# The z projection of a gated linear attention, from one pass over float32 operands to three over their float32r halves

## The chip, the cores and the metric

One core of one Trainium2 chip runs the whole program. The time is device microseconds of one execution; the kernel before has a median of 1250.59 us over 3 runs (1248.19 to 1251.07).

## What is computed

Two transformer layers over x of 4 x 256 tokens (T = 1024) and 256 channels. The change lies in the attention of the first layer, which has 16 heads of 128:

```python
q = _silu(x @ Wq); k = _silu(x @ Wk); v = _silu(x @ Wv)
z = x @ Wz                       # the change is here
q, k, v = (_causal_dwconv(u, w) for ...)     # 4 taps
# rotary, norms of q and k, 4 lags of q.k_s * sigmoid(a_s * b) * v_s
out = out * rms * norm_w * _silu(z)
return out @ Wout
```

Behind it come a feed-forward layer with weights from a table of 16 values, a second attention (softmax, 4-bit codes with scales) and a mixture of 32 experts.

## The kernel before

The program is written by hand, one instruction stream for each engine, with semaphores between them. Nothing plans the order: each stream runs as it stands in the code.

**Heads and turns.** The first attention goes head by head. `turns0` (line 350) calls `turn` on every engine; a turn of head h does part 1 (projections and convolutions of head h), part 2 (the scores and the sum over lags of head h-1) and part 3 (gate and store of head h-2). Two turns stand ahead of a hardware loop of 7 x 2, two or three behind it. The weights of one head are one tile `wh[par]` of 128 x 1024: four blocks q, k, v, z of KC x 128 = 256 columns.

**Two kinds of product.** TensorE multiplies a stationary tile (loaded first, the PEld rows of the profile) with moving columns. q, k and v are made channel by channel: stationary is a 128x128 block of weights, moving are 512 tokens. They go by halves: ScalarE writes the upper half of a tile as float32r (`upper0`, line 908: `w_hi`), VectorE subtracts it from the tile and so gets the lower half (`lower0`, line 1160: `w_lo`, in place over `wh`), the input has its two halves `hh_h` and `hh_l` once for all heads, and `by_halves` (lines 519 to 523) issues three products for one: low x high, high x low, high x high. These are lines 521, 522, 523 in the profile, whoever calls them.

z is made token by token: stationary is a 128x128 block of the input `h_t`, moving are the 128 columns of the z weights, for 8 blocks of tokens and KC = 2 halves of the channels, 16 float32 products for a head (line 609). The profile shows two records (a load and a multiplication each) for each float32 product, and one for each float32r product. z's columns of `wh` are no part of the halves: `w_hi` and `w_lo` hold QKV = 768 of the 1024 columns.

**TensorE's order in a turn**, with what it waits for: squared sums of k of head h-1 (line 576), k (waits for silu of z of the head before), the gate's transposes (595), v, a transpose of sums (604), z (609; waits for `a0_silu_k`), the transposes of v of head h-1 (616), its scores (624), squared sums of q (576), then `project_q` of head h+1, which waits for `a0_w_lo`, `a0_silu_v` and `a0_v_tok` (ScalarE has copied slot 0 of PSUM out, line 967), and last the products with the band (640, 644).

**ScalarE's order in a turn**: store of head h-2 (932, 938), silu and first tap of k (914, 924), 944, silu and tap of v, `upper0` of head h+1 (908), squares of q and k (955; wait for their convolutions), silu of z (959; waits for `a0_z`), `v_tok` of head h-1 (967; waits for the transposes of v and `a0_rqk`), silu and tap of q of head h+1.

**VectorE's order in a turn**: gate (1188), 1193, convolution of q (1171, three times), 1200 (waits for the transpose of line 604), convolution of k, `lower0` of head h+1 (1160), convolution of v, the band (1213, 1216), four rotary products (1177, 1183).

SyncE reloads `wh[par]` for head h+2 after `a0_z` of head h, and loads the table's indices after the last `a0_z`; they lie over `hh_h` and `hh_l`.

Of the kernel before, what the change touches and what calls it, by code (L numbers as in the profile page):

```python
# [5 lines left out]
ALU = mybir.AluOpType  # L6
ACT = mybir.ActivationFunctionType
AX = mybir.AxisListType
F32 = mybir.dt.float32
# [4 lines left out]
P = 128  # L14
B, S, D = 4, 256, 256
T = B * S
KC = D // P
# [21 lines left out]
QKV = 3 * KC * P  # L39
# [20 lines left out]
def build(nc, a, out, b_rows, code_rows):  # L60
# [7 lines left out]
    def sg(name):  # L68

        name = REUSED.get(name, name)  # L70
        if name not in named:
            named[name] = ctx.enter_context(nc.semaphore(name))
        return named[name]
# [30 lines left out]
    with ctx:  # L104
# [6 lines left out]
        x_t, h_t = sb("x_t", KC * T), sb("h_t", KC * T)  # L111
# [31 lines left out]
        arena, arena_r = twice("arena", ARENA)  # L143
# [3 lines left out]
        def carve(*sizes, base=0, of=arena):  # L147
            o, v = base, []
            for n in sizes:
                v.append(of[:, o:o + n])  # L150
                o += n
            assert o <= ARENA, o
            return v
# [8 lines left out]
        sw, rot, sqr = {"q": swq, "k": swk}, {"q": qr[:, 0:T], "k": kr}, {"q": sqq, "k": sqk}  # L162
        cv, sz, wh = [cv0, cv1], [sz0, sz1], [wh0, wh1]
        at_w = 3 * UW + 13 * T + TAPS + 3 * BAND + P + H * NT * TAPS
        wl0, _, wl1, _, w_hi0, w_hi1 = carve(QKV, KC * P, QKV, KC * P, QKV, QKV, base=at_w, of=arena_r)
        w_lo, w_hi = [wl0, wl1], [w_hi0, w_hi1]
        wmod = [G[:, 0:KC * 6 * D], G[:, KC * 6 * D:2 * KC * 6 * D]]
        ba_sb = G[0:2 * H, 2 * KC * 6 * D:2 * KC * 6 * D + T + PAD]
# [16 lines left out]
        hh_h, hh_l = lut_w_r[:, 0:KC * T], lut_w_r[:, KC * T:2 * KC * T]  # L185
# [11 lines left out]
            base=10 * T + RING * 2 * ROW + 4 * CAP + 4 * CAP + RING * 2 * D + T + D)  # L197
# [138 lines left out]
        def slot(i):  # L336
            return psum[:, i * T:i * T + T]
# [161 lines left out]
        def _(pe):  # L499
# [28 lines left out]
            for n in range(2):  # L528
                for k in range(KC):
                    i = nc.tensor.matmul(bank(4 + n)[0:2 * H, :], par_in[:, M_WBA + k * 2 * H:M_WBA + (k + 1) * 2 * H],  # L530
                                         h_t[:, k * T + n * 512:k * T + n * 512 + 512], start=(k == 0), stop=(k == KC - 1))
            i.then_inc(sg("ba_ps"), 1)
            pe.wait_ge(sg("ba_sb"), 2)
            for s in range(TAPS):
                for t in range(NT):
                    i = nc.tensor.transpose(lag_block(s)[:, t * 2 * H:t * 2 * H + 2 * H], ba_sb[:, t * P + s:t * P + s + P],
                                            ident[0:2 * H, 0:2 * H])
# [26 lines left out]
                i.then_inc(sg("a0_q"), 1)  # L564

            def turn(h, hh, par, st):
                def w(j, k):
                    return wh[par][:, (j * KC + k) * P:(j * KC + k) * P + P]

                def project0(dst, j, n):  # L570
                    return halves0(dst, par, j, n)

                def squared_sums(j, s):
                    for i in range(NT):
                        n = j * NT + i
                        m = nc.tensor.matmul(bank(7)[0:2 * NT, 0:P], select(n), sqr[s][:, i * P:i * P + P],  # L576
                                             start=(n == 0), stop=(n == 2 * NT - 1), skip_group_check=True)
                    return m

                if 2 in st:  # L580
                    pe.wait_ge(sg("a0_sq_k"), h)
                    squared_sums(1, "k").then_inc(sg("a0_ssq"), 1)
                if 1 in st:
                    if since(h, 1):
                        pe.wait_ge(sg("a0_silu_z"), h)
                    if since(h, 2):
                        pe.wait_ge(sg("a0_on_lo"), h - 1)
                    project0(slot(1), 1, 0)
                    if since(h, 2):
                        pe.wait_ge(sg("a0_on"), h - 1)  # L590
                    project0(slot(1), 1, 1).then_inc(sg("a0_k"), 1)
                if 3 in st:
                    pe.wait_ge(sg("a0_g"), h - 1)
                    for i in range(NT):
                        t = nc.tensor.transpose(g_block(i), sz[par][:, i * P:i * P + P], ident)
                    t.then_inc(sg("a0_gT"), 1)
                if 1 in st:
                    pe.wait_ge(sg("a0_silu_q"), h + 1)
                    for n in range(2):
                        i = project0(slot(0), 2, n)  # L600
                    i.then_inc(sg("a0_v"), 1)
                if 2 in st:
                    pe.wait_ge(sg("a0_rows_sb"), h)
                    nc.tensor.transpose(bank(7)[:, P:2 * P], rows_sb, ident).then_inc(sg("a0_ssqT"), 1)
                if 1 in st:
                    pe.wait_ge(sg("a0_silu_k"), h + 1)
                    for t in range(NT):
                        for k in range(KC):
                            i = nc.tensor.matmul(slot(1)[:, t * P:t * P + P], h_t[:, k * T + t * P:k * T + t * P + P],  # L609
                                                 w(3, k), start=(k == 0), stop=(k == KC - 1))  # L610
                    i.then_inc(sg("a0_z"), 1)
                if 2 in st:
                    pe.wait_ge(sg("a0_conv_v"), 3 * h)
                    pe.wait_ge(sg("a0_silu_v"), evens(h))
                    for i in range(NT):
                        t = nc.tensor.transpose(slot(0)[:, i * P:i * P + P], cv[1 - par][:, i * P:i * P + P], ident)
                    t.then_inc(sg("a0_vT"), 1)

                    pe.wait_ge(sg("a0_rope_q"), 32 * h)
                    pe.wait_ge(sg("a0_rope_k"), 32 * h)  # L620
                    if since(h, 2):
                        pe.wait_ge(sg("a0_gT_sb"), h - 1)
                    for i in range(NT):
                        m = nc.tensor.matmul(s_block(i), kr[:, i * P:i * P + P], qr[:, i * P:i * P + WIDE], start=True, stop=True)
                    m.then_inc(sg("a0_S"), 1)
                if 1 in st:
                    pe.wait_ge(sg("a0_sq_q"), h + 1)
                    if since(h, 1):
                        pe.wait_ge(sg("a0_ssq_s"), h)
                    squared_sums(0, "q")  # L630
                if 4 in st:
                    project_q(h + 1, 1 - par)
                if 2 in st:

                    pe.wait_ge(sg("a0_A"), h)
                    pe.wait_ge(sg("a0_v_tok"), h)
                    pe.wait_ge(sg("a0_silu_z"), evens(h))
                    for i in range(NT):
                        o = slot(1)[:, i * P:i * P + P]
                        m = nc.tensor.matmul(o, A[:, i * WIDE:i * WIDE + P], v_tok[:, i * P:i * P + P], start=True, stop=(i % 2 == 0),  # L640
                                             skip_group_check=True)
                        if i % 2:
                            c = (i - 1) * WIDE + P
                            m = nc.tensor.matmul(o[0:PAD, :], A[:, c:c + PAD], v_tok[:, (i - 1) * P:i * P], start=False,
                                                 stop=True, skip_group_check=True)
                    m.then_inc(sg("a0_o"), 1)
# [145 lines left out]
            for t in range(NT):  # L792
                for k in range(KC):
                    i = nc.tensor.matmul(bank(4)[:, t * E:t * E + E], xr[:, k * T + t * P:k * T + t * P + P],
                                         par_in[:, M_GW + k * E:M_GW + k * E + E], start=(k == 0), stop=(k == KC - 1))
            i.then_inc(sg("moe_logits"), 1)

            for t in range(NT):
                for k in range(KC):
                    i = nc.tensor.transpose(bank(t // 2)[:, (t % 2) * D + k * P:(t % 2) * D + k * P + P],  # L800
                                            xr[:, k * T + t * P:k * T + t * P + P], ident)
# [4 lines left out]
            for j in range(2):  # L806
                pe.wait_ge(*at("moe_xt", 2 * j + 2))
                for n in range(2):
                    for k in range(KC):
                        i = nc.tensor.matmul(bank(2 * j + n), wsh[:, k * D + j * P:k * D + j * P + P],  # L810
                                             xr[:, k * T + n * 512:k * T + n * 512 + 512], start=(k == 0), stop=(k == KC - 1))
# [3 lines left out]
            for s in range(NT):  # L815
                i = nc.tensor.matmul(bank(5)[:, s * E:NT * E], ones if s else strict, mk[:, 0:(NT - s) * E], start=(s == 0),
                                     stop=(s == NT - 1), skip_group_check=True)
# [76 lines left out]
        def _(act):  # L894
# [9 lines left out]
            def upper0(h, hh, par):  # L904
                act.wait_ge(sg(f"a0_w{par}"), 16 * (hh + 1))
                if since(h, 2):
                    act.wait_ge(sg("a0_v"), h - 1)
                nc.scalar.activation(w_hi[par], wh[par][:, 0:QKV], ACT.Copy).then_inc(sg("a0_w_hi"), 1)

            def silu_and_tap(h, w, s, dst):  # L910
                act.wait_ge(sg("a0_" + s), h + 1)
# [184 lines left out]
        def _(dve):  # L1096
# [60 lines left out]

            def lower0(h, par):
                dve.wait_ge(sg("a0_w_hi"), h + 1)
                nc.vector.tensor_tensor(w_lo[par], wh[par][:, 0:QKV], w_hi[par].bitcast(F32), ALU.subtract)\  # L1160
                    .then_inc(sg("a0_w_lo"), 1)

            lower0(0, 0)
# [518 lines left out]
```

## Time and profile before

| | |
|---|---|
| median of 3 runs | 1250.59 us |
| the profiled execution | 1246.91 us |
| its span, first to last instruction | 1245.1 us |
| TensorE busy in the span | 1070.6 us, 86% |
| VectorE, ScalarE, GpSimd busy | 745.7 us (60%), 539.2 us (43%), 294.3 us (24%) |
| chain that ended last: TensorE's share | 66%, VectorE 16%, ScalarE 6% |
| z of the first attention (line 609) | 512 records, 59.8 us busy |
| granted TensorE clock, mean of the span | 0.915 of 2.4 GHz |

The profiled execution took 1.8 us more than its span, and lies 3.7 us below the median of the runs. Busy times of one engine are unions of overlapping records, so a record's duration is longer than the step from its start to the next start. In the trace, times count from the start of the span.

### The profile page before, as it was taken

Reading aid. Unit: us, or ns where it says so; the run is one execution under the profiler, and the core shown is the slowest. Engines: PE = TensorE matmul, PEld = TensorE weight load, DVE = VectorE, ACT = ScalarE, POOL = GpSimd, SP = SyncE. Lnnn points to the kernel's source line nnn. Section 1 sums busy time; section 2 is a strip of 40 time slices with the busy share of each in tenths; the row PEclk is TensorE's granted clock in tenths of the full one; section 3 lists DMA queues with packets and bytes.
Section 4 is the critical chain, followed back from the end, with each engine's and each line's share of the span. In section 5 each row is a group of like instructions: output and inputs, shape, how many; then the busy total and the mean of one; then the engine's idle time right before and its main releaser. Section 6 shows DMA issues by size and latency. Waiting matters only on the chain.

```text
span 1245.1 us, 16986 instructions
## 1 busy us (share of the span) xinstructions
PE 1070.6 (86%) x5909; PEld 822.3 (66%) x5909; DVE 745.7 (60%) x1231; ACT 539.2 (43%) x1035; POOL 294.3 (24%) x244
## 2 busy tenths in 40 slices
PE   6799999999999959747967999999998968329996
PEld 4478888788788744323436899988984425128885
DVE  1378888878878828952136777778772034303344
ACT  1157677677667648910005555555551011002320
POOL 0013333333233220021002111111100000546660
PEclk8599999999999979978988999999998987759997
DMA  7046676676677650070001111111001000148954
GB/s 247 2 109 163 141 149 146 148 148 137 163 144 160 167 135 17 1 185 1 0 1 51 52 51 31 45 51 51 25 0 51 1 13 1 76 161 261 274 169 177
DMA packets 73016, 121.53 MB, mean 98 GB/s; under 512 B 24771, under 2 KB 50062, under 8 KB 72208
## 3 DMA queue, kind: packets, MB, share of 16 engines
q1 hardware_dynamic: 60944, 86.91, 22.9%
q0 software_dynamic: 12032, 34.11, 14.1%
q8 instruction: 23, 0.38, 0.1%
q14 instruction: 17, 0.14, 0.0%
HBM read 70.31 MB, written 38.08 MB: 87 GB/s over the span
## 4 chain that ended last, share of the span: by engine, by line
PE 66%; DVE 16%; ACT 6%; issue 5%; POOL 4%; DMA 2%; DVEq 0%; POOLq 0%; ACTq 0%; SPq 0%
PE psum L521 7%; PE psum L523 7%; PE psum L522 7%; PE psum L759 5%; PE psum L661 4%; PE psum L847 4%; PE psum L544 3%; PE psum L609 3%; PE psum L640 3%; PE psum L732 3%; ACT arena L967 2%; PE psum L255 2%; DVE arena L1171 2%; PE psum L857 2%; POOL slot_rows L1593 2%
## 5 line engine op out<-in xcount | busy, mean ns | idle before, releaser
L1171 DVE SCALAR_TENSOR_TENSOR arena<-arena,par_in 128x1024 f32<-128x1024 f32 x144 | 184.4, 1282 | 19.2 <-ACT arena L924 7.8
L521 PE MATMUL psum<-lut_w_r,arena_r 128*128 128x512 f32 x320 | 132.4, 414 | 23.3 <-POOL arena_r L1570 10.1
L522 PE MATMUL psum<-lut_w_r,arena_r 128*128 128x512 f32 x320 | 128.0, 400 | 0.0
L523 PE MATMUL psum<-lut_w_r,arena_r 128*128 128x512 f32 x320 | 128.0, 400 | 0.0
L661 PE MATMUL psum<-G,arena 128*128 128x512 f32 x256 | 112.1, 600 | 2.7 <-DVE G L1362 1.5
L1554 POOL DMA_DIRECT2D arena<-arena x64 | 53.8, 983 | 187.4 <-DVE arena L1183 187.1
L1015 ACT ACTIVATE arena<-psum,small 128x256 f32<-128x256 f32 x128 | 59.4, 474 | 86.0 <-DVE small L1310 86.0
L661 PEld LDWEIGHTS psum<-G,arena 128*128 128x128 f32 x256 | 49.1, 193 | 64.5 <-issue 64.5
L521 PEld LDWEIGHTS psum<-lut_w_r,arena_r 128*128 128x128 f32 x320 | 61.3, 191 | 43.4 <-issue 23.2
L914 ACT ACTIVATE arena<-psum 128x1024 f32<-128x1024 f32 x48 | 49.3, 1027 | 81.2 <-PE psum L523 81.2
L292 POOL TENSOR_TENSOR small<-small 128x8 f32<-128x8 f32 x6 | 9.9, 1646 | 313.1 <-DVE small L283 287.7
L521 PE MATMUL psum<-arena_r 128*128 128x256 f32 x256 | 77.8, 304 | 1.5 <-DVE arena_r L1335 1.5
L1548 POOL TENSOR_TENSOR small<-small 128x16 f32<-128x16 f32 x16 | 62.2, 3888 | 60.7 <-DVE small L1200 60.7
L1601 POOL DMA_INDIRECT out_rows<-arena x64 | 62.7, 980 | 46.3 <-DVE arena L1455 24.1
L523 PE MATMUL psum<-arena_r 128*128 128x256 f32 x256 | 73.5, 287 | 0.0
L522 PE MATMUL psum<-arena_r 128*128 128x256 f32 x256 | 73.5, 287 | 0.0
L1570 POOL TENSOR_TENSOR arena_r<-arena,arena_r 128x512 fp32r<-128x512 f32 x16 | 21.2, 1325 | 217.3 <-ACT arena_r L1026 217.3
L523 PEld LDWEIGHTS psum<-lut_w_r,arena_r 128*128 128x128 f32 x320 | 61.1, 191 | 14.7
L522 PEld LDWEIGHTS psum<-lut_w_r,arena_r 128*128 128x128 f32 x320 | 61.3, 192 | 11.4
L759 PE MATMUL psum<-arena,h_t 128*128 128x128 f32 x512 | 62.2, 275 | 0.0
L759 PEld LDWEIGHTS psum<-arena,h_t 128*128 128x128 f32 x512 | 60.7, 192 | 1.5 <-DVE arena_r L1328 0.2
L576 PE MATMUL psum<-arena,cst 128*16 128x128 f32 x512 | 61.3, 273 | 0.4 <-ACT arena L955 0.4
(200 smaller groups left out, 2317.0 us busy)
## 6 DMA issues: line engine op xcount, KB each, us to landing
arena<-arena POOLq DMA_DIRECT2D x64, 256.0 KB, 5.5
arena<-in_w_moe SPq DMA_DIRECT2D x32, 384.0 KB, 3.9
slot_rows<-nowhere SPq DMA_DIRECT2D x16, 576.0 KB, 4.8
arena<-slot_rows SPq DMA_DIRECT2D x32, 288.0 KB, 3.9
arena<-bands SPq DMA_DIRECT2D x16, 528.0 KB, 3.5
arena<-in_w_qkvz SPq DMA_DIRECT2D x16, 512.0 KB, 3.8
sq_rows<-arena POOLq DMA_DIRECT2D x16, 512.0 KB, 7.2
arena<-in_qkv_codes SPq DMA_DIRECT2D x16, 384.0 KB, 3.2
```

The costliest lines, as they stand in the source:

```text
L521: nc.tensor.matmul(dst, w_l, x_h, start=start, stop=False, skip_group_check=True)
L522: nc.tensor.matmul(dst, w_h, x_l, start=False, stop=False, skip_group_check=True)
L523: return nc.tensor.matmul(dst, w_h, x_h, start=False, stop=stop, skip_group_check=True)
L576: m = nc.tensor.matmul(bank(7)[0:2 * NT, 0:P], select(n), sqr[s][:, i * P:i * P + P], start=(n == 0), stop=(n == 2 * NT - 1), skip_group_c ...
L661: i = nc.tensor.matmul(bank(2 * m + n), w[:, h * D + m * P:h * D + m * P + P], G[:, h * T + n * 512:h * T + n * 512 + 512], start=(h == 0) ...
L759: i = nc.tensor.matmul(slot(0)[:, t * P:t * P + P], h_t[:, k * T + t * P:k * T + t * P + P], w(2, k), start=(k == 0), stop=(k == KC - 1))
L847: i = nc.tensor.matmul(bank(2 + 2 * (e % 2) + j)[:, 0:CAP], we[e % WRING][:, k * D + j * P:k * D + j * P + P], xT[e % 2][:, k * CAP:(k + 1 ...
L1015: e = nc.scalar.activation(prob[b % 2][:, i * S:i * S + S], bank(4 + b % 2)[:, i * S:i * S + S], ACT.Exp, bias=nmax[:, 2 * b + i:2 * b + i ...
L1171: nc.vector.scalar_tensor_tensor(by_batch(dst), by_batch(u[s])[:, :, j:j + S], par_in[:, bass.ds(M_CW + (w * H + h) * TAPS + j, 1)], by_ba ...
L1548: nc.gpsimd.tensor_tensor(rqk[1 - par], ssq_s, neg_half, ALU.pow).then_inc(sg("a0_rqk"), 1)
L1554: nc.gpsimd.dma_start(rot[s][to:to + 64, :], sw[s][of:of + 64, :], accum_op=ALU.add)\
L1601: nc.gpsimd.indirect_dma_start(out_rows, bass.IndirectOffsetOnAxis(place.bitcast(I32)[:, c:c + 1], 0), eo[e % RING][:, r * D:(r + 1) * D], ...
```

## The change

z goes by halves as q, k and v do. The upper and lower halves now hold all 1024 columns of a head's weights; ScalarE's copy and VectorE's difference cover 1024 columns where they covered 768. z stays token by token: each of its 16 products becomes three, with a half of the input stationary and 128 columns of a half of the weights moving, 48 for a head. The wait in `upper0` goes from `a0_v` to `a0_z` of head h-1, since z is now the last reader of the halves.

```diff
-        wl0, _, wl1, _, w_hi0, w_hi1 = carve(QKV, KC * P, QKV, KC * P, QKV, QKV, base=at_w, of=arena_r)
+        wl0, wl1, w_hi0, w_hi1 = carve(*[4 * KC * P] * 4, base=at_w, of=arena_r)
...
             def turn(h, hh, par, st):
-                def w(j, k):
-                    return wh[par][:, (j * KC + k) * P:(j * KC + k) * P + P]
-
...
                     for t in range(NT):
                         for k in range(KC):
-                            i = nc.tensor.matmul(slot(1)[:, t * P:t * P + P], h_t[:, k * T + t * P:k * T + t * P + P],
-                                                 w(3, k), start=(k == 0), stop=(k == KC - 1))
+                            c, w = slice(k * T + t * P, k * T + t * P + P), slice((3 * KC + k) * P, (3 * KC + k) * P + P)
+                            i = by_halves(slot(1)[:, t * P:t * P + P], hh_h[:, c], hh_l[:, c], w_hi[par][:, w], w_lo[par][:, w],
+                                          k == 0, k == KC - 1)
                     i.then_inc(sg("a0_z"), 1)
...
             def upper0(h, hh, par):
                 act.wait_ge(sg(f"a0_w{par}"), 16 * (hh + 1))
                 if since(h, 2):
-                    act.wait_ge(sg("a0_v"), h - 1)
-                nc.scalar.activation(w_hi[par], wh[par][:, 0:QKV], ACT.Copy).then_inc(sg("a0_w_hi"), 1)
+                    act.wait_ge(sg("a0_z"), h - 1)
+                nc.scalar.activation(w_hi[par], wh[par], ACT.Copy).then_inc(sg("a0_w_hi"), 1)
...
             def lower0(h, par):
                 dve.wait_ge(sg("a0_w_hi"), h + 1)
-                nc.vector.tensor_tensor(w_lo[par], wh[par][:, 0:QKV], w_hi[par].bitcast(F32), ALU.subtract)\
+                nc.vector.tensor_tensor(w_lo[par], wh[par], w_hi[par].bitcast(F32), ALU.subtract)\
                     .then_inc(sg("a0_w_lo"), 1)
```

The first place is TensorE in the second turn, from the end of v (its last product, line 523) to what follows z. Operands are named moving first, stationary second. Before:

```order
L523 MATMUL psum<-lut_w_r,arena_r 128x512
L604 MATMUL psum<-cst,arena 128x128
L609 MATMUL psum<-arena,h_t 128x128 x16
L616 MATMUL psum<-cst,arena 128x128 x8
L624 MATMUL psum<-arena 128x132 x8
L576 MATMUL psum<-arena,cst 16x128 x8
```

After the change, the same place up to the first three products of z (the lines behind 609 have moved up by two or three; `lut_w_r` holds the halves of the input):

```order
L523 MATMUL psum<-lut_w_r,arena_r 128x512
L601 MATMUL psum<-cst,arena 128x128
L521 MATMUL psum<-arena_r,lut_w_r 128x128
L522 MATMUL psum<-arena_r,lut_w_r 128x128
L523 MATMUL psum<-arena_r,lut_w_r 128x128
```

The last three rows come 16 times, and then follow line 614 (the transposes of v) and the rest as before. Nothing else moved on TensorE.

The second place is VectorE in the same turn, from the convolution of k over `lower0` to the band. Before:

```order
L1200 TENSOR_SCALAR small<-psum 128x16
L1171 SCALAR_TENSOR_TENSOR arena<-arena,par_in 128x1024 x3
L1160 TENSOR_TENSOR arena_r<-arena,arena_r 128x768
L1171 SCALAR_TENSOR_TENSOR arena<-arena,par_in 128x1024 x3
L1213 TENSOR_TENSOR arena<-psum,arena 128x792
```

After:

```order
L1198 TENSOR_SCALAR small<-psum 128x16
L1169 SCALAR_TENSOR_TENSOR arena<-arena,par_in 128x1024 x3
L1158 TENSOR_TENSOR arena_r<-arena,arena_r 128x1024
L1169 SCALAR_TENSOR_TENSOR arena<-arena,par_in 128x1024 x3
L1211 TENSOR_TENSOR arena<-psum,arena 128x792
```

The order is the same; the difference is wider by 256 columns. ScalarE's copy (line 908, now 906) is wider by as much, at its old place.

## Rows read from the trace of the kernel before

**Rows 1.** The page: the chain that ended last, by engine

```profile
PE 66%; DVE 16%; ACT 6%; issue 5%; POOL 4%; DMA 2%; DVEq 0%; POOLq 0%; ACTq 0%; SPq 0%
```

**Rows 2.** Chain of waits, one turn of the loop to the next z: start us, us, what

```profile
186.44 3.57 PE psum L609 x32
...
191.77 1.01 ACT arena L959
192.77 2.08 ACT arena L967 x8
...
194.99 0.47 PE psum L521
...
210.17 3.57 PE psum L609 x32
```

**Rows 3.** TensorE in order of time, same turn: start us, us, engine, line, [idle before <-releaser]

```profile
192.63 1.92 PE L576 MATMUL psum<-arena,cst 128*16 128x128 f32 x16
194.99 0.47 PE L521 MATMUL psum<-lut_w_r,arena_r 128*128 128x512 f32 x1 [0.43 <-ACT arena L967]
...
201.47 1.91 PE L576 MATMUL psum<-arena,cst 128*16 128x128 f32 x16
203.31 0.50 PE L521 MATMUL psum<-lut_w_r,arena_r 128*128 128x512 f32 x1
```

**Rows 4.** ScalarE in order of time, same turn

```profile
190.80 1.06 ACT L955 ACTIVATE arena<-arena 128x1024 f32<-128x1024 f32 x1 [0.44 <-DVE arena L1171]
```

**Rows 5.** Waits of TensorE's multiplications, 62 to 423.4 us: total us, times, longest

```profile
PE psum L521 <- DVE arena_r L1160: 6.9, 1, 6.9
PE psum L521 <- ACT arena L967: 6.3, 14, 0.9
PE psum L576 <- ACT arena L955: 0.4, 1, 0.4
```

**Rows 6.** Groups of weight loads by form: busy us, mean ns of one

```profile
L522 PEld LDWEIGHTS psum<-lut_w_r,arena_r 128*128 128x128 f32 x320 | 61.3, 192 | 11.4
...
L609 PEld LDWEIGHTS psum<-arena,h_t 128*128 128x128 f32 x512 | 58.5, 192 | 1.5
...
L576 PEld LDWEIGHTS psum<-arena,cst 128*16 128x16 f32 x512 | 48.3, 97 | 8.8 <-ACT arena L955 0.6 <-issue 0.4
```

**Rows 7.** Float32 loads for 4 moving columns (line 506): duration min/median/max, first to last start

```profile
L506 PEld LDWEIGHTS psum<-small,G x23: 190/192/192, 14.4 to 16.9; 128*128 128x128 f32 x23
```

**Rows 8.** Float32r products: chain at 512 columns (186 us) and at 256 (807 us)

```profile
185.86 0.23 PE psum L522
186.10 0.23 PE psum L523
...
807.13 0.12 PE psum L521
807.25 0.12 PE psum L522
```

**Rows 9.** Stretches: us, busy (records) of PE, PEld, DVE, ACT, POOL, then PEclk, DMA, GB/s

```profile
14.50:17.00 2.50, 2.50 (x25) 2.50 (x23) 2.25 (x2) 0.99 (x1) 0.00 (x0) 1.00 0.41 125
36.00:46.00 10.00, 10.00 (x49) 10.00 (x47) 4.94 (x10) 0.00 (x0) 0.37 (x5) 0.50 0.00 0
186.00:210.00 24.00, 23.57 (x160) 19.63 (x159) 19.59 (x19) 16.54 (x29) 8.21 (x6) 1.00 0.69 150
```

**Rows 10.** Copies and differences by line and form: x count, busy us, mean ns

```profile
L908 ACT ACTIVATE arena_r<-arena 128x768 fp32r<-128x768 f32 x16 | 13.2, 827 | 0.0
L975 ACT ACTIVATE lut_w_r<-h_t 128x1024 fp32r<-128x1024 f32 x2 | 2.0, 1040 | 0.0
L1155 DVE TENSOR_TENSOR lut_w_r<-h_t,lut_w_r x2: 1218/1221/1224, 59.6 to 60.7; 128x1024 fp32r<-128x1024 f32 x2
L1160 DVE TENSOR_TENSOR arena_r<-arena,arena_r 128x768 fp32r<-128x768 f32 x16 | 15.2, 951 | 0.0
```

**Rows 11.** TensorE's wait in the last turn with a z, 423.4 to 436 us

```profile
PE psum L640 <- DVE arena L1216: 1.1, 1, 1.1
```

## The prediction

> **What bounds the kernel now.** I read the page first: TensorE has 66% of the chain that ended last [rows 1]. Then the chain of waits in one turn of the loop: z stands in it with 32 records and 3.57 us, and the next z starts 210.17 - 186.44 = 23.73 us after it, which is the length of a turn; behind z come ScalarE's lines 959 and 967, and then TensorE's line 521, the q of the next head [rows 2]. What the reader must see is that two paths run side by side between the transpose of line 604 and that q. TensorE itself does z, the transposes, the scores of line 624 and the squared sums of line 576. VectorE and ScalarE do the convolution of k, its square, silu of z and the eight copies of line 967. TensorE waits at the end: 0.43 us in this turn [rows 3], 6.3 us in 14 turns [rows 5]. So the other path is a little the longer one, and ScalarE's part of it starts where VectorE releases the second square of line 955 [rows 4], not where z ends. Elsewhere in the turn TensorE has no gap: in 24 us it is busy 23.57 at the full clock of 2.4 GHz, granted 1.00 [rows 9]. The turn is bound by TensorE with half a microsecond of air in it.
>
> **What the 16 float32 products cost.** 32 records in 3.57 us are 111.6 ns from start to start [rows 2]. The columns are not what sets that. Line 506 loads a 128x128 stationary tile too but moves 4 columns: 23 loads start between 14.4 and 16.9 us, 2.5 us / 22 = 114 ns at the full clock, and at half the clock (0.50, 1.2 GHz) 47 to 49 of the same records fill 10.0 us, some 208 ns each, or 104 at twice the clock [rows 7, 9]. A float32 load of 128 columns thus occupies TensorE's load path about 104 to 114 ns, and a record of 128 columns can't be shorter.
>
> **What the 48 float32r products will cost.** The trace has no float32r product under 256 columns, so this is bounded by neighbours. The load of a float32r tile takes 192 ns in its rows, exactly as long as that of a float32 tile, while a tile of 16 columns takes 97 [rows 6]: 95 ns for 112 columns, 0.85 ns each, 109 ns for 128. So the float32r load is as slow as the float32 one. At 512 and 256 columns float32r products start 233 and 120 ns apart [rows 8]; there the columns cover the load. At 128 columns they don't: a line through the two points gives 120 - 128 x 0.44 = 63 ns, under the 109 of the load. I take 111.6 ns, the step of float32 records whose load has the same length, as nearest in tile and columns; the ends are 63 ns (the load somehow hidden) and 120 ns (the 256-column row, if its 120 are a load with something on top and not columns). 48 x 111.6 = 5.36 us for a head in place of 3.57: **+1.79 us a head**. Three passes in place of four buy nothing, since a load is paid for each product: 48 loads where 32 were.
>
> The Trainium skill (TensorE: Matmul & The Clock Gate, Weight-path perf modes) speaks against this: fast weight load is on where there are 128 weights and the type isn't FP32, and the page's sustained figure for 128 columns is about 81 ns per product. By that 48 products would take an estimated 3.9 us, +0.3 us a head, and the sum would be no change. The 192 ns in the float32r load's row speak against it, since a faster load would be shorter than the float32 one.
>
> **What the turn makes of it.** 1.79 us more on TensorE's path first fill its wait. The recorded wait is 6.3 us over 14 turns, plus 0.4 once at line 576 [rows 5]. The first q product also starts late by the step from line 576: 2.36 us after its start with the wait, 1.84 without [rows 3], so the wait is nearer 0.52 than 0.43, some 1.3 us more over 14 turns. Together 8.0 us are filled. Could ScalarE become the bound in TensorE's place? z ends 1.79 us later; its silu at 191.77 started some 1.7 us after z ended [rows 2], so it moves by about 0.1, while TensorE reaches q 1.3 us later: no.
>
> 15 of the 16 heads lie ahead of that or the next q. In the last turn with a z TensorE waits 1.1 us at line 640 for VectorE [rows 11], and what ends there last is the rotary part on VectorE and its DMA; 0.7 us of TensorE's extra reach line 640 and nothing behind waits for it. I cost that one at nothing.
>
> Sum: 15 x 1.79 - 8.0 = **18.8 us**.
>
> **The wider copies.** ScalarE's copy goes from 827 to about 1040 ns, the row of the same copy at 1024 columns; VectorE's difference from 951 to about 1221 [rows 10]. ScalarE's +0.21 us stand ahead of the squares; it waits 0.44 us for VectorE there [rows 4], which covers it, and if that cover were gone TensorE's later arrival covers it too. VectorE's +0.27 us stand behind the convolution of k, off the path to the squares; behind it VectorE has idle time in every turn (19.59 of 24 us busy [rows 9]). Only the first difference, ahead of the loop, is waited for by TensorE alone, the 6.9 us [rows 5]: +0.27 us. The wait of `upper0` for z of the head before in place of v is over 20 us old when it is asked, 0. No DMA is added: the halves lie where the weights lay.
>
> Sum of all: 18.8 + 0.3 = 19.1 us, on the profiled execution's 1246.9: 1266.0. The runs' median is 3.7 us higher, so against it **1250.6 + 19.1 = 1269.7, say 1270 us**. With 120 ns a product it is 48 x 0.12 = 5.76, +2.19 a head, 15 x 2.19 - 8.0 + 0.3 = 25.2: 1276. Of the differences an experiment can tell, 0.3% is about 3.8 us.
>
> **Rivals.**
>
> (a) *The loads are hidden, columns decide.* At 63 ns z takes 3.0 us, 0.5 less than now. Then the path over VectorE and ScalarE is the bound, TensorE waits 1.0 us where it waited 0.5, and the time stays: 1250.6 + 0.3 + at most a second 0.27 for the first turn, 1251. For it: the line through the two float32r rows. Against it: the equal 192 ns of the loads.
>
> (b) *Faster.* As (a), but the chain is right in putting z's end ahead of lines 959 and 967 [rows 2], so that a shorter z lets ScalarE, and so q, start earlier. The place is the wait of line 959 for z; it decides from z shorter than 3.57 us, that is under 74 ns a product. Price: 15 x 0.54 = 8 us at 63 ns, 1242. The Trainium skill (FP8 and Floating Point Precision) says true FP32 takes four passes through the array; by three passes for four z would be an estimated 2.7 us, and the gain 13 us. Against (b): the gap of 0.44 in ScalarE's rows ahead of the second square [rows 4], which is released by VectorE.
>
> (c) *A narrow float32r product runs at the rate of a float32 one*, two records' worth, 223 ns each. Nothing in the trace excludes it, as no such product is there; at 256 columns it isn't so [rows 8]. 48 x 0.223 = 10.7 us, +7.1 a head, 15 x 7.14 - 8.0 + 0.3 = 99: 1350.
>
> (d) *TensorE's extra is absorbed more than I think*, a wait on the other path that I misread: with twice the filled time, 1262. It belongs to the forecast's own range.
>
> **How the numbers follow.** The forecast, load-bound at 112 to 120 ns, has 0.82; (a) 0.07; (b) 0.03; (c) 0.08. The forecast's range runs from 1262, twice the absorbed wait, to 1285, for 120 ns plus another 10 ns a product (48 x 0.01 x 15 = 7 us) and the runs' own spread. That holds the time 8 times in 10, since the other three have 0.18 together. Faster by over 0.3%: (b), 0.03. Within 0.3%: (a), 0.07. Slower: 0.90.
>
> **What the profile of the changed kernel would show.** Lines 521 to 523 get a form of 128x128 with 256 records each, 768 in all. Right: they start 110 to 120 ns apart, z takes 5.3 to 5.8 us of a turn, the wait of line 521 for ScalarE's copies is gone, and two turns lie some 25.0 us apart where it was 23.73. Loads of about 192 ns that start one right behind the other would be the cause itself. Wrong: a step near 63 ns (then the wait at line 521 grows to about 1 us), or near 220. If z takes 5.4 us and the turn is not longer by 1.3, my account of the wait is wrong. Copies of 1.04 and differences of 1.22 us with no new wait of TensorE on them confirm the rest; a wait of q's products for VectorE's line 1158 in the loop would refute it.

## The result, and the profile after

| | before | after |
|---|---|---|
| median of 4 runs | 1249.78 us (1248.19 to 1251.07) | 1266.28 us (1262.13 to 1270.73) |
| ratio to before | | 1.0133, 95% interval 1.0096 to 1.0170 |
| profiled execution | 1246.91 us | 1266.34 us |
| its span | 1245.1 us | 1264.5 us |
| TensorE busy | 1070.6 us | 1095.9 us |
| TensorE's share of the chain | 66% | 72% |

The change makes the kernel 1.3% slower, 16.5 us by the medians and 19.4 by the two profiled executions; 19.1 was forecast, and 1270 us for the median. The changed kernel was run again later, with 18 runs of the kernel before on the same chip, and gave a ratio of 1.0156 (1.0120 to 1.0193); by the medians that is 1259.65 against 1243.26 us, 16.4 us.

The groups of TensorE and of its weight loads, by line and form, that stand in the place of line 609 (busy us, mean ns):

```profile
L521 PE MATMUL psum<-arena_r,lut_w_r 128*128 128x128 f32 x256 | 70.9, 277 | 0.0
L523 PE MATMUL psum<-arena_r,lut_w_r 128*128 128x128 f32 x256 | 70.5, 275 | 0.0
L522 PE MATMUL psum<-arena_r,lut_w_r 128*128 128x128 f32 x256 | 70.4, 275 | 0.0
...
L522 PEld LDWEIGHTS psum<-arena_r,lut_w_r 128*128 128x128 f32 x256 | 49.1, 192 | 0.0
```

768 records, as the form said, and each load takes 192 ns, as in [rows 6]. The chain of waits over one z of the changed kernel (start us, us, what) has the step:

```profile
187.28 0.11 PE psum L601
...
191.69 0.11 PE psum L521
191.81 0.11 PE psum L522
191.92 0.11 PE psum L523
192.03 0.11 PE psum L521
192.14 0.11 PE psum L522
192.25 0.11 PE psum L523
...
192.70 0.90 PE psum L614 x8
```

z lies between the end of line 601's transpose at 187.39 and 192.70: 5.31 us in the chain, 48 steps of 111 ns. Before it was 3.57 [rows 2]. Each of the three lines has its own load for each product, although lines 522 and 523 use the same stationary tile one behind the other (`hh_h` in `by_halves`); their step is the same 111 ns. The chain no longer leaves TensorE behind z. In order of time TensorE shows the turn and its end:

```profile
187.12 0.27 PE L601 MATMUL psum<-cst,arena 128*128 128x128 f32 x1
...
195.35 1.92 PE L573 MATMUL psum<-arena,cst 128*16 128x128 f32 x16
197.20 0.50 PE L521 MATMUL psum<-lut_w_r,arena_r 128*128 128x512 f32 x1
...
212.14 0.27 PE L601 MATMUL psum<-cst,arena 128*128 128x128 f32 x1
```

The turn is 212.14 - 187.12 = 25.02 us (before 23.73), and q starts 1.85 us after line 573 where it was 2.36 [rows 3], with no wait in front of it. TensorE's waits from 58 to 440 us are one row, where [rows 5] had three:

```profile
PE psum L521 <- DVE arena_r L1158: 7.1, 1, 7.1
```

ScalarE and VectorE in the same turn, in order of time:

```profile
189.54 1.04 ACT L906 ACTIVATE arena_r<-arena 128x1024 fp32r<-128x1024 f32 x1
190.49 1.04 ACT L953 ACTIVATE arena<-arena 128x1024 f32<-128x1024 f32 x1
191.76 1.06 ACT L953 ACTIVATE arena<-arena 128x1024 f32<-128x1024 f32 x1 [0.23 <-DVE arena L1169]
...
191.64 1.22 DVE L1158 TENSOR_TENSOR arena_r<-arena,arena_r 128x1024 fp32r<-128x1024 f32 x1
```

The copy takes 1.04 us and the difference 1.22; the copy has eaten half of ScalarE's wait of 0.44 [rows 4] and no more.

**Where the 19.4 us of the two profiles lie.** VectorE's first convolution starts at 70.88 us before and 66.25 after, and the first one in the last turn with a z, 15 heads on, at 418.53 before and 432.64 after:

```profile
66.25 3.93 DVE L1169 SCALAR_TENSOR_TENSOR arena<-arena,par_in 128x1024 f32<-128x1024 f32 x3 [7.71 <-ACT arena L922]
...
432.64 3.91 DVE L1169 SCALAR_TENSOR_TENSOR arena<-arena,par_in 128x1024 f32<-128x1024 f32 x3
```

That is 347.65 us before and 366.39 after: 15 turns cost 18.7 us. (The hardware loop of this attention holds 6 x 2 turns, with two ahead and four behind; the 7 x 2 told ahead of the prediction is the second attention's.) Ahead of the 15 turns the changed kernel was 4.6 us quicker, behind them 5.3 slower.

Of the 5.3 us, 0.6 is the change's: the z of the last head. Between the transposes of sums ahead of it and behind it lie 17.78 us before and 18.41 after (18.42 in the later profile of the changed kernel, and 17.78 in the experiment below whose z is as long as before). TensorE in order of time, before and after:

```profile
423.19 0.27 PE L604 MATMUL psum<-cst,arena 128*128 128x128 f32 x1
440.97 0.27 PE L604 MATMUL psum<-cst,arena 128*128 128x128 f32 x1
...
437.32 0.27 PE L601 MATMUL psum<-cst,arena 128*128 128x128 f32 x1
455.73 0.27 PE L601 MATMUL psum<-cst,arena 128*128 128x128 f32 x1
```

The rest is no larger than what one program scatters: the later profile of the changed kernel had turns of 25.02 us again, but 824.9 us from the same convolution to its end where this one had 831.9. Ahead of the turns a part of the scatter is TensorE's clock among the small products of the beginning: 48 products of line 506 took 7.66 us in the chain of the kernel before and 5.26 in that of the changed one, by how much of them fell to 1.2 GHz.

```profile
13.96 5.26 PE psum L506 x48
```

That is 2.4 of the 4.6 us; what is left was not taken apart. So the 19.4 us of the profiles lie close to the forecast in part because two scatters of about 5 us cancel; the 18.7 us of the turns are the number to hold against it.

### The profile page after: what moved, and what is told of

Its sections match the earlier page's. It is cut to its first block, busy times and chain, and to the rows that moved or that the text cites. A ratio compares the mean times of both kernels' runs of the same rounds, so it can differ in the third digit from the quotient of the medians.

```text
span 1264.5 us, 17498 instructions
## 1 busy us (share of the span) xinstructions
PE 1095.9 (87%) x6165; PEld 847.6 (67%) x6165; DVE 747.4 (59%) x1231; ACT 544.6 (43%) x1035; POOL 295.7 (23%) x244
## 4 chain that ended last, share of the span: by engine, by line
PE 72%; issue 11%; DVE 11%; ACT 2%; DMA 2%; POOL 1%; DVEq 0%; another core or an unknown queue 0%; SPq 0%; POOLq 0%; ACTq 0%
PE psum L521 10%; PE psum L523 9%; PE psum L522 9%; PE psum L757 5%; PE psum L845 4%; PE psum L659 4%; PE psum L573 4%; PE psum L544 4%; PE psum L638 3%; PE psum L730 3%; PE psum L622 2%; PE psum L855 2%; DVE arena L1266 2%; PE psum L676 2%; PE psum L642 2%
## 5 line engine op out<-in xcount | busy, mean ns | idle before, releaser
L1169 DVE SCALAR_TENSOR_TENSOR arena<-arena,par_in 128x1024 f32<-128x1024 f32 x144 | 184.4, 1282 | 19.1 <-ACT arena L922 7.7
L521 PE MATMUL psum<-arena_r,lut_w_r 128*128 128x128 f32 x256 | 70.9, 277 | 0.0
L523 PE MATMUL psum<-arena_r,lut_w_r 128*128 128x128 f32 x256 | 70.5, 275 | 0.0
L522 PE MATMUL psum<-arena_r,lut_w_r 128*128 128x128 f32 x256 | 70.4, 275 | 0.0
```

The lines of the kernel that those rows point to most:

```text
L521: nc.tensor.matmul(dst, w_l, x_h, start=start, stop=False, skip_group_check=True)
L522: nc.tensor.matmul(dst, w_h, x_l, start=False, stop=False, skip_group_check=True)
L523: return nc.tensor.matmul(dst, w_h, x_h, start=False, stop=stop, skip_group_check=True)
L1169: nc.vector.scalar_tensor_tensor(by_batch(dst), by_batch(u[s])[:, :, j:j + S], par_in[:, bass.ds(M_CW + (w * H + h) * TAPS + j, 1)], by_ba ...
```

## The experiments

The theory: each product on TensorE pays the load of its stationary tile, 112 ns for 128 columns in float32r as in float32; 128 columns or fewer are hidden behind it. And beside TensorE runs a path over VectorE and ScalarE that keeps a turn at 23.7 us. The rivals are a narrow float32r product that is slow by its own columns, and a chain in which silu of z starts when z ends. All times of this section stand against runs of the kernel before on the same chip, whose level there was 1241.7 to 1246.5 us.

**Half the moving columns.** Each product moves 64 columns; half of z is left out.

```diff
-...slice((3 * KC + k) * P, (3 * KC + k) * P + P)
+...slice((3 * KC + k) * P, (3 * KC + k) * P + 64)
-by_halves(slot(1)[:, t * P:t * P + P], hh_h[:, c], ...
+by_halves(slot(1)[:, t * P:t * P + 64], hh_h[:, c], ...
```

> z's 48 products move 64 columns in place of 128, with the same 128x128 stationary tiles; half of z is not computed. Theory (each product pays its weight load, columns are hidden): the step stays 111.7 ns, z 5.36 us, the turn 25.0 us, the time that of the changed kernel, about 1266 us. Rival (narrow float32r products run at half the column rate, 128 columns in 107 to 112 ns): the step falls to about 56 ns, z to 2.7 us, the turn to 23.7 us where the other path binds, the time to about 1250 us.

One line's records in one z: durations min/median/max, first to last start.

```profile
L523 PEld LDWEIGHTS psum<-arena_r,lut_w_r x16: 192/192/192, 178.8 to 183.8; 128*128 128x128 f32 x16
L523 PE MATMUL psum<-arena_r,lut_w_r x16: 276/277/277, 178.8 to 183.8; 128*128 128x64 f32 x16
```

5.0 us from the first to the 16th, 45 steps: 111 ns, as with 128 columns. The rival's 56 ns are out. But the time was 1298.7 us in a single run, not 1266: 57 us over the kernel before on the same chip, where the changed kernel costs 16 to 19, and 39 us over the changed kernel of the later runs. That was not expected. The turns that stay at the full clock take 25.0 us here too; others take 26.7 to 29.9. From the first transpose of sums to the last one there are 401.4 us where the changed kernel has 368.7, so 33 of the 39 us lie in these turns. There the granted clock falls to 0.50 for 3 to 10 us at a time, 13 times in 16 heads, each time 2.6 to 5.8 us after the start of a z that is itself 5.3 us long. Stretches of busy time: a z, the 3 us behind it, and most of the next turn (us, busy of PE, PEld, DVE, ACT, POOL, PEclk, DMA, GB/s):

```profile
202.50:208.50 6.00, 6.00 (x51) 5.72 (x50) 5.06 (x6) 5.29 (x6) 3.96 (x1) 1.00 0.31 60
209.00:212.00 3.00, 3.00 (x15) 3.00 (x16) 2.79 (x3) 1.98 (x5) 0.00 (x0) 0.50 0.45 134
212.50:235.50 23.00, 23.00 (x158) 19.20 (x156) 16.60 (x17) 14.30 (x23) 8.21 (x6) 1.00 0.63 128
```

TensorE is busy all the time by its records, and yet it is at 1.2 GHz from 209 to 212 us, behind a stretch of 48 loads that each moved 64 columns. In the changed kernel, with 128 columns in the same slots, the granted clock is 1.00 over all 15 turns. The span's mean clock was 0.892 against 0.920.

**A quarter of the stationary columns.** Each product loads 32 columns of the input and moves 128; three quarters of z are left out.

```diff
-c, w = slice(k * T + t * P, k * T + t * P + P), ...
+c, w = slice(k * T + t * P, k * T + t * P + 32), ...
-by_halves(slot(1)[:, t * P:t * P + P], hh_h[:, c], ...
+by_halves(slot(1)[0:32, t * P:t * P + P], hh_h[:, c], ...
```

> z's 48 products load 32 stationary columns in place of 128 and move 128 columns as before; three quarters of z is not computed. Theory (the load is the cost): the load shrinks to about 27 ns (0.85 ns a column), the step falls to the column rate, 55 to 65 ns, z to about 3.0 us, the turn to 23.7 us with a wait of about 1 us at q, the time to about 1250 us. Rival (narrow products at half the column rate): the step stays at 107 to 112 ns, the turn at 25.0 us, the time at 1266 us.

```profile
L523 PEld LDWEIGHTS psum<-arena_r,lut_w_r x16: 107/108/112, 182.2 to 184.9; 128*32 128x32 f32 x16
L523 PE MATMUL psum<-arena_r,lut_w_r x16: 220/223/228, 182.2 to 184.9; 128*32 128x128 f32 x16
```

2.7 us over 45 steps: 60 ns. The same products with the same moving columns run in about half the time once the load is short: the load's record is 108 ns long where it was 192. The time was 1238.8 us, 2.9 under the median before on that chip; a single run can't be told from it. TensorE's largest wait from 62 to 423 us:

```profile
PE psum L521 <- ACT arena L965: 14.4, 13, 1.1
```

The wait has grown from 6.3 us in 14 turns [rows 5] to 14.4 in 13, and z's saving of 0.7 us a turn has gone into it. In the 14th turn the wait stands at line 573 instead (1.3 us), and once the scores wait 2.0 us for a DMA.

**Two products.** The product of the input's low half is left out, 32 loads a head.

```diff
-i = by_halves(slot(1)[...], hh_h[:, c], hh_l[:, c], w_hi[par][:, w], w_lo[par][:, w], k == 0, k == KC - 1)
+nc.tensor.matmul(slot(1)[...], hh_h[:, c], w_lo[par][:, w], start=(k == 0), stop=False, skip_group_check=True)
+i = nc.tensor.matmul(slot(1)[...], hh_h[:, c], w_hi[par][:, w], start=False, stop=(k == KC - 1), skip_group_check=True)
```

> z from two products in place of three, 32 a head: low half of the input left out. Copies and differences stay 1024 columns wide. Theory: 32 loads of 111.7 ns are 3.57 us, as the 32 records of before; the wider copies are hidden but for 0.3 us: 1250 us, ratio to before 1.000, turn 23.7 us. Rival (the wider copy on ScalarE or difference on VectorE lies on the path): up to 0.5 us a turn, turn 24.2 us, 1257 us.

1242.09 us against 1241.67, ratio 1.0015 (0.9988 to 1.0042). The turns are 23.73 us long, and TensorE's wait is as before:

```profile
PE psum L521 <- ACT arena L967: 6.6, 14, 0.9
```

32 float32r loads cost what 32 float32 records did, and the wider copy and difference cost nothing that 19 and 10 runs can tell. The +0.3 us I gave the first difference lies inside the interval of the times; by the traces it is there, as TensorE's one wait for it ahead of the loop is 7.1 us here against 6.9 [rows 5].

**One product.** High by high alone, 16 loads a head; both low parts are left out.

```diff
-i = by_halves(slot(1)[...], hh_h[:, c], hh_l[:, c], w_hi[par][:, w], w_lo[par][:, w], k == 0, k == KC - 1)
+i = nc.tensor.matmul(slot(1)[...], hh_h[:, c], w_hi[par][:, w], start=(k == 0), stop=(k == KC - 1))
```

> z from one product, high half by high half, 16 a head; both low parts left out. Theory (beside TensorE a path over VectorE's convolution of k and ScalarE's squares, silu of z and copies of v binds, and z's end does not start it): z takes 1.79 us, the turn stays at 23.7 us, the wait at q grows to about 2.3 us, the time is 1250 us, no gain over two products. Rival (silu of z starts when z ends, as the chain of waits had it): the turn falls by the 1.79 us saved to 21.9 us and the time to about 1224 us.

```profile
PE psum L521 <- ACT arena L965: 30.3, 14, 2.3
PE psum L573 <- ACT arena L953: 2.5, 1, 2.5
```

1246.82 us, ratio 1.0045 (1.0016 to 1.0074): the saving of 1.8 us a turn went whole into the wait (30.3 us in place of 6.3), so silu of z is not started by z's end, and the rival's 1224 us is out. It is even 5 us slower than before, which I had not expected. In the profile one piece of it shows: TensorE works less, and once in the loop its clock falls behind such a wait, where the kernel before stays at 1.00 (stretches as above):

```profile
306.40:309.40 3.00, 1.37 (x13) 0.97 (x10) 2.86 (x3) 3.00 (x9) 0.00 (x0) 1.00 0.99 287
310.00:313.00 3.00, 2.99 (x7) 2.43 (x8) 3.00 (x4) 0.00 (x0) 0.00 (x0) 0.50 0.00 0
```

That one turn is 1.4 us longer than the others (25.16 us against 23.74). The rest of the 5 us was not taken apart, so its cause is open.

**Four products.** Low by low added, 64 loads a head.

> The changed kernel with a fourth product, low by low, 64 a head. Theory: 16 loads more of 111.7 ns are 1.79 us more a turn, and nothing is left to absorb them: turn 26.8 us, 16 x 1.79 = 29 us over the changed kernel, about 1288 us where that takes 1260. Rival (the products' columns or PSUM accumulation and not the loads): the fourth product has the stationary tile of none of its neighbours and costs the same by that too, so this run tells only whether the cost stays linear.

1287.5 us in a single run, with a single 1246.45 for the kernel before beside it: +41.1. The kernel with three products had +16.4 in its later runs, so 16 loads more in each head are 24.7 us by that, 29 expected; the changed kernel's four first runs ranged over 8.6 us. By the loop, a turn went from 25.02 to 26.81 us, 1.79 as expected, and TensorE waits for nothing from 62 to 460 us. One premise of the expectation is wrong: the fourth product has the same stationary tile (`hh_l`) as the product of line 521 behind it. It costs its 112 ns all the same, as line 523 does behind 522.

**The changed kernel once more.**

> The changed kernel itself, on one chip with the kernel before: the turn is 25.02 us against 23.73, 15 turns give 19 us, so 1.5% over the kernel before, whatever the level of the chip. If the ratio is under 1.011, part of the 19 us is given back outside the turns.

1259.65 against 1243.26 us, 1.0156 (1.0120 to 1.0193). Turn 25.02 us. The ratio lies over 1.011, so nothing says that part of it is given back outside the turns; by the medians it is 16.4 us, which the interval (15 to 24 us) holds too.

**The kernel before without the second path.** On ScalarE the copies of v come ahead of silu of z; on TensorE the transpose of line 604 goes between the halves of v.

```diff
 # ScalarE, in turn
-                    act.wait_ge(sg("a0_z"), h + 1)
-                    ...
-                    nc.scalar.activation(sz[par], slot(1), ACT.Silu).then_inc(sg("a0_silu_z"), 1)
                 if 2 in st:
                     act.wait_ge(sg("a0_vT"), h)
...
                     m.then_inc(sg("a0_v_tok"), 1)
+                if 1 in st:
+                    act.wait_ge(sg("a0_z"), h + 1)
+                    ...
+                    nc.scalar.activation(sz[par], slot(1), ACT.Silu).then_inc(sg("a0_silu_z"), 1)
 # TensorE, in turn
-                    for n in range(2):
-                        i = project0(slot(0), 2, n)
-                    i.then_inc(sg("a0_v"), 1)
+                    project0(slot(0), 2, 0)
                 if 2 in st:
                     pe.wait_ge(sg("a0_rows_sb"), h)
                     nc.tensor.transpose(bank(7)[:, P:2 * P], rows_sb, ident).then_inc(sg("a0_ssqT"), 1)
+                if 1 in st:
+                    project0(slot(0), 2, 1).then_inc(sg("a0_v"), 1)
```

> The kernel before with two moves: ScalarE does the copies of v (v_tok) ahead of silu of z, and TensorE the transpose of the sums between the two halves of v. Nothing is computed otherwise. Theory (a path over VectorE and ScalarE sets the end of the turn by 0.5 us): the moves take 1.0 and 0.6 us from it, TensorE binds alone, the wait at q goes, the turn falls to 23.2 us, the time by 15 x 0.5 = 8 us, 0.6%. Rival (TensorE was the bound already): no change.

1236.04 against 1243.26 us, ratio 0.9944 (0.9923 to 0.9965). TensorE's waits from 62 to 423 us are down to two rows, and two squared sums lie a turn apart:

```profile
PE psum L576 <- ACT arena L955: 0.4, 1, 0.4
PE psum L624 <- DMA arena<-arena: 0.2, 1, 0.2
...
204.82 1.92 PE L576 MATMUL psum<-arena,cst 128*16 128x128 f32 x16
...
228.06 1.92 PE L576 MATMUL psum<-arena,cst 128*16 128x128 f32 x16
```

The turn is 23.24 us, 0.49 less. That is the air in the turn that the forecast counted as 0.52.

**z channel by channel.** Weights stationary, 512 tokens moving, 12 products a head. z then comes with channels on the partitions; the attention's output is transposed ungated and VectorE multiplies it with norm weight and gate in one pass. The ungated output lies in `h_t`, which nothing reads any more in this stage.

```diff
-                    for t in range(NT):
-                        for k in range(KC):
-                            ...
+                    for n in range(2):
+                        i = project0(slot(1), 3, n)
...
-                        t = nc.tensor.transpose(g_block(i), sz[par][:, i * P:i * P + P], ident)
+                        t = nc.tensor.transpose(g_block(i), chunk(h_t, par)[:, i * P:i * P + P], ident)
...
-                    nc.scalar.activation(G[:, bass.ds((h - 2) * T, T)], psum[:, 4 * 512:4 * 512 + T], ACT.Copy, ...)
-                    nc.vector.tensor_tensor(sz[par], G[:, bass.ds((h - 2) * T, T)], sz[par], ALU.mult)
+                    nc.vector.scalar_tensor_tensor(G[:, bass.ds((h - 2) * T, T)], psum[:, 4 * 512:4 * 512 + T],
+                                                   par_in[:, bass.ds(M_NW + h - 2, 1)], sz[par], ALU.mult, ALU.mult)
```

> z by halves too, but channel by channel: stationary are the weights, moving 512 tokens, 12 products a head in place of 48 of 128 columns; the gate is multiplied after the transposes, by VectorE in one pass with the norm weight, which takes the place of its product and of ScalarE's copy. Theory: at 233 ns a product z is 2.80 us against 5.36, TensorE's work falls to 22.5 us a turn, but the other path holds the turn at 23.7 us: the time is that of the kernel before (ratio 1.000), 19 us under the changed kernel, with a wait of about 1.3 us at q. Rival (there is no second path): turn 22.5 us, 19 us under the kernel before.

1240.88 against 1243.26 us, ratio 0.9992 (0.9972 to 1.0013): z is 12 steps of 233 ns, and the time is that of the kernel before. Its waits and its squared sums:

```profile
PE psum L521 <- ACT arena L957: 16.4, 14, 1.2
...
202.57 1.91 PE L573 MATMUL psum<-arena,cst 128*16 128x128 f32 x16
...
226.32 1.91 PE L573 MATMUL psum<-arena,cst 128*16 128x128 f32 x16
```

The turn is 23.75 us with a wait of 1.2 at q, as said.

**Both together**: channel by channel z and the two moves of the second path.

> The channel by channel z with the two moves on ScalarE and TensorE. Theory: both paths are shortened, TensorE binds at about 22.5 us a turn, 15 x 1.25 = 19 us under the kernel before, ratio 0.985. If another wait takes over (the rotary DMA ahead of the scores, or VectorE's new product between the convolutions), the turn stays over 23 us.

```profile
206.03 1.92 PE L573 MATMUL psum<-arena,cst 128*16 128x128 f32 x16
...
228.61 1.92 PE L573 MATMUL psum<-arena,cst 128*16 128x128 f32 x16
```

1221.67 against 1243.26 us, ratio **0.9841** (0.9811 to 0.9872), with a turn of 22.58 us. This version beats both kernels: 1.6% under the one before, about 3% under the changed one.

## Why the prediction was right

*The load sets the step.* Forecast 111.6 ns from the float32 neighbours with the 4-column row as floor; measured 111. 64 moving columns left it at 111, 32 stationary ones brought it to 60. So what I had only from the length of the load's row is shown from both sides. The low end of 63 ns was the column rate itself, and it is what a short load gives. The high end of 120 was columns too: at 256 they pass the load.

One reading behind it was too short. Of the float32 records I said that the columns are not what sets their 111.6 ns. The chain of the kernel before shows otherwise:

```profile
201.64 1.75 PE psum L576 x16
...
947.79 55.19 PE psum L661 x128
```

Line 576 loads only 16 columns [rows 6] and moves 128: 1.75 us / 16 = 109 ns a record. Line 661 moves 512, also at a granted 1.00: 55.19 / 128 = 431 ns, so an estimated 108 for 128. A float32 record of 128 columns thus takes about 110 ns by its columns as well as by its load, and a shorter load would not have helped it. A float32r product moves its columns in half that time (60 ns), and only there is the load alone the bound. The forecast's 111.6 ns was taken from a row in which both are equal, and stands because the load is the same for both types.

The fast weight load that the Trainium skill (TensorE: Matmul & The Clock Gate, Weight-path perf modes) names for types other than FP32 isn't seen in these float32r loads: 192 ns each here. The section LDWEIGHTS (loading the stationary operand) of the same page of the Trainium skill gives the load as columns divided by 1.2 GHz, an estimated 107 ns for 128 columns. The steps of 111 agree with it.

*+1.79 us a head, of which 0.5 is absorbed.* Forecast 15 x 1.79 - 8.0 = 18.8 us; the 15 turns took 18.7 more. The last head's z, costed at nothing, took 0.6 more: TensorE's wait of 1.1 us at line 640 [rows 11] covers only a part of its 1.79, and what reached that line was handed on to the next turn, against what I had said of it. The absorbed part, which I had put together from a recorded wait and a late start, is shown by itself: shortening the second path in the kernel before gave 0.49 us a turn.

*The path over VectorE and ScalarE.* Rival (b) rested on a chain that ran from z over silu of z to q. One product in place of two shortened z by 1.8 us, to half its length before, and left the turn at 23.7: the chain's step from TensorE to ScalarE there was no cause, and the idle row in front of the second square was the right one to read. Rival (a) would have met the same floor.

*Rival (c)*, a narrow product at the rate of a whole float32 one, had only the 256-column rows against it and fell with the first profile.

*The wider copies.* 1.04 and 1.22 us as their rows said, hidden in the loop. The 0.3 us for the one ahead of the loop can't be told from the times, but TensorE's wait for the first difference is 6.9 us in both profiles with 768 columns and 7.1 to 7.2 in all nine with 1024.

*What the sum didn't hold.* The clock. The forecast took for granted that the 15 turns stay at 2.4 GHz, and they do. That was luck in part: with 64 columns in the same slots the clock fell 13 times and the turns took 33 us more, and with one product it fell once, for 1.4 us. Nothing in the prediction asked for a reason why it should hold here.

## What to carry to other kernels

Count loads, not passes: every float32 or float32r record read here with a 128x128 stationary tile stood about 110 ns or more before the next at the full clock, even where that one had the same tile. A float32 product of 128 moving columns is two such steps, three products of halves are three, so the change made z half as long again. At 512 columns the load is hidden (233 ns a product). If a projection must be narrow, ask whether the other operand can be the moving one and the consumer turned round instead. And before costing a change on the engine with the largest share, look at its waits inside the turn: half a microsecond of air absorbed over a quarter of the loss, and behind it the second path swallowed the whole of the gain where z was made shorter.

## What was not expected of the hardware

The granted clock of TensorE can fall while its records leave no gap. With 48 loads of 128 columns and 64 moving columns each, it went to 1.2 GHz in or right behind 13 of 16 z's, for 3 to 10 us at a time, and the kernel took 1298.7 us in its single run where 128 moving columns at the same step take 1260 to 1266. With 16 products in place of the 32 records of before, TensorE waited 2.3 us a turn, its clock fell once in the loop, and the kernel was 0.45% slower than the one before (0.16 to 0.74). So leaving out half of the moving columns, or half of the products, made neither kernel faster. Of the first loss the clock accounts for most; of the second, 5 us, it accounts for 1.4, and the rest is open.
